# Two fused convolution blocks: raw images in place of normalised ones, and one expert added by an accumulating DMA

## The reference, cut to what matters

```python
def cond_conv(x):                      # x: the group-normalised input
    pooled = mean(x, axis=(2, 3))
    routing = sigmoid(pooled @ w_route.T + b_route)      # (16, 4)
    y = conv3x3(x, w_experts)                            # 4 experts, 128 -> 128
    out = einsum('beohw,be->bohw', y, routing)
    return silu(batch_norm(out))
x = x + cond_conv(group_norm(x))                         # 32 groups of 4 channels
x = x + conv3x3(group_norm(x), sign(W))
```

## Time and profile before

| | us |
|---|---|
| median of 3 runs | 273.05 (272.96 to 273.5) |
| profiled execution, its own time | 273.31 |
| span of its trace | 271.5 |
| PE, DVE, ACT, POOL busy | 264.0, 255.3, 219.6, 43.5 |

### The profile page before, as it was taken

The page is one execution under the profiler, slowest core; times in us unless marked ns, Lnnn a source line. Parts: engine busy times, 40 slices in busy tenths (PEclk is TensorE's granted clock), DMA queues, the critical chain, the costliest instruction groups (busy, mean ns, idle before and its releaser), DMA issues.

```text
span 271.5 us, 4138 instructions
## 1 busy us (share of the span) xinstructions
PE 264.0 (97%) x1339; PEld 183.0 (67%) x1339; DVE 255.3 (94%) x466; ACT 219.6 (81%) x450; POOL 43.5 (16%) x63
## 2 busy tenths in 40 slices
PE   8899999999999999999999999999999999999993
PEld 8544856758485766859586675848576685858663
DVE  5899999999999999999999999999999999995985
ACT  2489988998979798897979799897979895735870
POOL 3011020312112021212112021211202121210110
PEclk9999999999999999999999999999999999999999
DMA  7998836453726545261735545271645536272507
GB/s 215 417 374 304 303 140 154 62 115 72 141 80 96 138 78 154 34 123 78 126 109 77 154 63 121 69 138 77 100 135 77 154 38 121 81 134 97 77 2 155
DMA packets 10245, 35.20 MB, mean 130 GB/s; under 512 B 1264, under 2 KB 1904, under 8 KB 10224
## 3 DMA queue, kind: packets, MB, share of 16 engines
q0 software_dynamic: 4176, 15.21, 33.3%
q1 hardware_dynamic: 5616, 19.34, 18.7%
q10 hardware_dynamic: 432, 0.39, 0.4%
HBM read 11.34 MB, written 16.25 MB: 102 GB/s over the span
## 4 chain that ended last, share of the span: by engine, by line
PE 87%; DVE 8%; ACT 2%; issue 1%; POOL 1%; DVEq 0%; POOLq 0%
PE pc L590 40%; PE pb L555 14%; PE pa L555 14%; PE pe_ L555 13%; DVE U L1163 3%; PE pd L484 2%; PE pd L545 1%; POOL rstd L441 1%; PE ps L524 1%; PE ps L528 1%; DVE e_rows L1194 0%; ACT xn L869 0%; DVE lo L1285 0%; DVE U L1153 0%; DVE even L1172 0%
## 5 line engine op out<-in xcount | busy, mean ns | idle before, releaser
L1163 DVE SCALAR_TENSOR_TENSOR U<-we,route,U 128x1152 f32<-128x1152 f32 x45 | 63.6, 1412 | 0.6
L590 PE MATMUL pc<-lo,ws 128*128 128x496 f16 (+3 forms) x270 | 62.0, 375 | 0.0
L590 PE MATMUL pc<-hi,ws 128*128 128x496 f16 (+3 forms) x270 | 59.8, 375 | 0.5 <-ACT hi L930 0.5
L590 PEld LDWEIGHTS pc<-hi,ws 128*128 128x128 f16 x270 | 26.4, 98 | 30.0 <-issue 0.9
L590 PEld LDWEIGHTS pc<-lo,ws 128*128 128x128 f16 x270 | 27.7, 106 | 26.3
L555 PE MATMUL pb<-V,UM 128*128 128x256 f32 (+1 forms) x180 | 40.6, 375 | 0.6 <-DVE UM L1183 0.6
L555 PE MATMUL pe_<-V,U 128*128 128x256 f32 (+1 forms) x180 | 40.6, 375 | 0.0
L555 PE MATMUL pa<-V,UM 128*128 128x256 f32 (+1 forms) x180 | 40.5, 374 | 0.0
L555 PEld LDWEIGHTS pb<-V,UM 128*128 128x128 f32 x180 | 34.0, 190 | 5.9 <-issue 1.1
L441 POOL TENSOR_TENSOR rstd<-ve,nhalf 128x2 f32<-128x2 f32 (+1 forms) x19 | 15.4, 811 | 139.6 <-ACT ve L845 116.1
L555 PEld LDWEIGHTS pe_<-V,U 128*128 128x128 f32 x180 | 34.1, 190 | 3.8
(11 more groups left out here) (165 smaller groups left out, 408.8 us busy)
## 6 DMA issues: line engine op xcount, KB each, us to landing
X<-x SPq DMA_DIRECT2D x15, 512.0 KB, 5.3
out<-X SPq DMA_DIRECT2D x15, 512.0 KB, 2.6
out<-ev POOLq DMA_DIRECT2D x15, 512.0 KB, 5.5
X<-y POOLq DMA_DIRECT2D x14, 512.0 KB, 4.5
we<-w_experts SPq DMA_DIRECT2D x2, 768.0 KB, 8.4
ws_raw<-w_sign SPq DMA_DIRECT2D x1, 576.0 KB, 10.8
we<-w_experts SPq DMA_DIRECT2D x1, 512.0 KB, 6.4
out<-X SPq DMA_DIRECT2D x1, 384.0 KB, 2.8
```

The source lines that it names most:

```text
L590: mm = mm_(rows[:, r0 - first // W:r1 - first // W, c0:c1], ws[:, tap * C:(tap + 1) * C], plane((hi, lo)[part], i)[:, r0 + ky - 1:r1 + ky ...
L1163: v.scalar_tensor_tensor(out=nine(U[i % RING]), in0=expert(e), scalar=route[:, i, e:e + 1], in1=nine(U[i % RING]), op0=ALU.mult, op1=ALU.a ...
```

## The change

The normalised image is no longer made from image 1 on. The transform reads the raw image from `X`, which now has a row above and below each image; ACT fills these two rows with the group mean (`pads`), and the one point in which the mean does not cancel gets six times the mean added (`centring`). The scale (rstd) goes into the routes, which become rstd x (tanh + 1), with a factor of 0.5 in the batch norm's scale. From image 2 on ACT scales expert 1 into a new tile `scaled` (`scale_second`), POOL issues an accumulating DMA that adds it to `U` (`add_scaled`), and DVE's first mix is that of expert 2 and waits for that DMA. ACT's order becomes: `centring` and `pads` ahead of `hi`, and, behind the SiLU, the statistics of the next image first and then `routing`, `mix` and `scale_second`. In the head the statistics of image 1 move from DVE to ACT, `pool_routes(2)` moves ahead of `mix(1, 3)`, and some small PE products change places.

```diff
-        X = sb("X", [C, B * HW])
+        X = sb("X", [C, B, PH, W])
+        scaled = sb("scaled", [C, K * KCO])
-        xn = [sb(f"xn{p}", [C, PH, W]) for p in range(RING)]
+        xn = sb("xn", [C, PH, W])
...
+        def first_mix(i):
+            return 2 if i >= SCALED_FROM else 1
...
+            def add_scaled(i):
+                pool.wait_ge(mix_first, firsts_before(i) + 1)
+                pool.wait_ge(scaled_ready, i - SCALED_FROM + 1)
+                g.dma_start(flat(U[i % RING][:]), scaled[:], accum_op=ALU.add).then_inc(scaled_added, 16)
...
+            add_scaled(SCALED_FROM)
             for t in range(1, B + 1):
                 power(t + LAG - 1)
                 if 0 <= t - 2 < B - LATE:
                     add_output(t - 2)
                 if ND <= t < B and t not in DVE_RESIDUAL:
                     residual(t)
+                if t + LAG - 1 < B:
+                    add_scaled(t + LAG - 1)
...
+            def centring(i):
+                if in_one(i):
+                    act.wait_ge(gvar_ready, i + 1)
+                else:
+                    act.wait_ge(gnm_ready, gnm_chain(i))
+                for n, factor in enumerate((1.0, P1_SUM)):
+                    activation(centre[:, i, n:n + 1], gnm(i, IN), ACT.Copy, scale=-factor).then_inc(centre_ready, 1)
+            def pads(i):
+                act.wait_ge(centre_ready, 2 * i)
+                activation(X[:, i, 0:PH:PH - 1, :], ones[:, 0:2 * W].rearrange("p (a w) -> p a w", a=2), ACT.Copy,
+                           scale=centre[:, i, 0:1]).then_inc(pads_ready, 1)
...
+            def scale_second(i):
+                wait(act, scaled_added, 16 * (i - SCALED_FROM))
+                activation(scaled[:].rearrange("p (g n) -> p g n", n=C), expert(1), ACT.Copy,
+                           scale=route[:, i, 1:2]).then_inc(scaled_ready, 1)
...
             var_in(3)
+            routing(2)
+            mix(2)
+            scale_second(2)
             silu(0)
             mean_mid(0)
-            routing(2)
-            mix(2)
             squares(LAG)
             add_variance(LAG, IN)
+            sign_weights()
             var_mid(0)
...
                 deviation(c)
+                if c < B:
+                    centring(c)
+                    pads(c)
                 bias(c, MID)
                 split_hi(t - 1)
                 if c < B:
-                    bias(c, IN)
                     pooled_plane(c)
                 split_hn(t - 1)
...
-                if c < B:
-                    normalise(c)
                 if t > 1:
                     silu(t)
                 if 1 < t < B - 1:
                     mean_mid(t)
                 if c + 1 < B:
                     mean_in(c + 1)
-                if c < B:
-                    routing(c)
-                    mix(c)
                 if c + 1 < B:
                     var_in(c + 1)
                 if c + 1 < CHAINS - 1:
                     squares(c + 1)
                 if c + 1 < B:
                     add_variance(c + 1, IN)
+                if c < B:
+                    routing(c)
+                    mix(c)
+                    scale_second(c)
...
-                if e == 1:
+                if e < first_mix(i):
+                    return
+                if e > first_mix(i):
+                    dve.wait_ge(mixed, mixes_before(i) + e - first_mix(i))
+                elif e == 1:
                     dve.wait_ge(mix_first, firsts_before(i) + 1)
                 else:
-                    dve.wait_ge(mixed, mixes_before(i) + e - 1)
+                    dve.wait_ge(scaled_added, 16 * (i - SCALED_FROM + 1))
...
             mix(1, 1)
             mix(1, 2)
+            pool_routes(2)
             mix(1, 3)
-            pool_routes(2)
...
                 if t > 1:
-                    mix(t + 1, 1)
+                    mix(t + 1, 2)
                 inverse_sums(t)
                 inverse_inner(t)
                 inverse_outer(t)
+                if t == 1:
+                    mix(t + 1, 2)
                 pool_routes(t + LAG - 1)
-                if t == 1:
-                    mix(t + 1, 1)
                 low_part(t - 1)
-                mix(t + 1, 2)
                 mix(t + 1, 3)
```

More of the change, by code:

```diff
@@ L33 @@
 K_ZERO, K_INF = -1.5, -6.0
+P1_SUM = 6.0
 G0, G2, G1 = 0, 1, 2
@@ L56 @@
 RING = 3
+SCALED_FROM = 2
 QUARTERS = 4
@@ L127, in build @@
         wroute = sb("wroute", [C, E])
-        parts = {i: sb(f"parts{i}", [C, n, 6]) for i, n in ((0, QUARTERS), (1, 2))}
-        agg = {i: sb(f"agg{i}", [C, 2]) for i in (0, 1)}
+        parts = {i: sb(f"parts{i}", [C, n, 6]) for i, n in ((0, QUARTERS),)}
+        agg = {i: sb(f"agg{i}", [C, 2]) for i in (0,)}
         first_d = sb("first_d", [C, 1])
@@ L277, in mixes_before @@
         def mixes_before(t):
-            return len(DIRECT_PARTS) * (E - 1) * min(t, ND) + (E - 1) * rank(t)
+            return len(DIRECT_PARTS) * (E - 1) * min(t, ND) + sum(E - first_mix(i) for i in range(ND, t))
+        def first_mix(i):
+            return 2 if i >= SCALED_FROM else 1
         def firsts_before(t):
@@ L457, in _ @@
              .then_inc(gdist_ready, 1)
-            for p in range(RING):
-                g.memset(xn[p][:, 0:PH:PH - 1, :], 0.0).then_inc(zeroed, 1)
+            g.memset(xn[:, 0:PH:PH - 1, :], 0.0).then_inc(zeroed, 1)
             g.memset(epsilon[:, 1:2], GN_EPS / LAST_SCALE ** 2).then_inc(zeroed, 1)
@@ L876, in routing @@
                 act.wait_ge(th_ready, i + 1)
-                activation(route[:, i, :], th[:, i, :], ACT.Copy, bias=0.5, scale=0.5).then_inc(route_ready, 1)
+                if i < ND:
+                    activation(route[:, i, :], th[:, i, :], ACT.Copy, bias=0.5, scale=0.5).then_inc(route_ready, 1)
+                else:
+                    act.wait_ge(rstd_ready, i + 1)
+                    activation(route[:, i, :], th[:, i, :], ACT.Identity, bias=rstd[:, i, IN:IN + 1],
+                               scale=rstd[:, i, IN:IN + 1]).then_inc(route_ready, 1)
             def mix(i):
@@ L948, in last_hi @@
                                scale=rstd[:, c, MID:MID + 1]).then_inc(last_hi_ready, 1)
-                activation(last_rest(hi), xn[1][:, LAST_ROWS:H + 1, :], ACT.Copy,
+                activation(last_rest(hi), xn[:, LAST_ROWS:H + 1, :], ACT.Copy,
                            scale=rstd[:, c, MID:MID + 1]).then_inc(last_hi_ready, 1)
@@ L980, in _ @@
             mix_first_part(0, 1)
+            mean_in(1)
             mix_first_part(0, 2)
+            var_in(1)
             deviations(1)
+            centring(1)
             mix_first_part(0, 3)
+            pads(1)
             variance(1)
-            bias(1, IN)
             pooled_plane(1)
-            normalise(1)
+            mean_in(2)
             routing(1)
             mix(1)
-            mean_in(2)
             var_in(2)
             deviations(2)
-            sign_weights()
+            centring(2)
+            mean_in(3)
+            pads(2)
             variance(2)
-            mean_in(3)
-            bias(2, IN)
             pooled_plane(2)
-            normalise(2)
             var_in(3)
+            routing(2)
+            mix(2)
+            scale_second(2)
             silu(0)
             mean_mid(0)
-            routing(2)
-            mix(2)
             squares(LAG)
             add_variance(LAG, IN)
+            sign_weights()
             var_mid(0)
@@ L1201, in inner_rows @@
                     return
-                rows = lambda first: xn[i % RING][:, first:first + H, :].rearrange("p (t k) w -> p t (k w)", k=TROWS)
+                rows = lambda first: X[:, i, first:first + H, :].rearrange("p (t k) w -> p t (k w)", k=TROWS)
                 v.tensor_tensor(f_rows[:].rearrange("p t k w -> p t (k w)"), rows(2)[:, :, W:3 * W],
@@ L1407, in _ @@
                     mix_part(part, x)
-            part_stats(1, 1)
-            aggregate(1)
-            columns(1)
+            bn_factor()
+            bn_scales()
+            bn_offset()
             for x in (1, 2, 3):
                 mix_part(2, x)
-            bn_factor()
-            mix_part(3, 1)
-            bn_scales()
-            mix_part(3, 2)
+            for x in (1, 2, 3):
+                mix_part(3, x)
             pool_routes(1)
-            mix_part(3, 3)
-            bn_offset()
             all_rows(1)
```

62 lines of the change are left out of this document (32 added, 30 removed).

## The result

The changed kernel takes 299.75 us (median of 4 runs, 298.44 to 301.09); the kernel before took 273.15 us beside it (272.96 to 273.5). The ratio is 1.0967, with an interval of 1.095 to 1.0985: 9.7% slower. The profiled execution took 299.47 us, its span is 297.7 us, 26.2 more than before.

A forecast was written before the change was run, and what follows sets the result against it. PE bounds the kernel before at 15.5 us per image; a DMA ring of 17.17 us would replace it. Twelve rounds put PE's late ps 19.1 us later, giving 292.4 us on the profiled execution, 292 as median; range 284 to 308.

The forecast's parts named there:

- What bounds: Kernel before: PE works 15.50 of 15.50 us per image, DVE 15.21, ACT 13.85; PE's head waits total 1.14 us.
- the ring: Scaled tile, POOL's DMA, DVE's mix and inverse transform, ACT up to the next scaled tile: 17.17 us per round.
- The landing: Accumulating DMA from issue to landing: 4.8 us taken, between 4.5 and 4.95; 6.2 us as upper bound.
- The routes: ACT's routes instructions between its mean pass and its mix, within the round: 0.44 us.
- The sum: From SiLU of image 1 through twelve rounds to PE's late ps at 267.5 us, 19.1 us later than before: 292 us.
- the eleven rounds: Eleven of the twelve rounds up to the mix of image 15, expert 2: 17.17 us each.
- the start: First DVE mix of expert 2 that waits for the DMA, image 3: starts at 51.25 us.
- the last, shorter round: Twelfth round, without mean and variance pass because there is no image 16: 14.87 us.
- What would show it: Signs: pb about 17.2 us apart, DVE idle 2 to 3 us, PE about 1.5 at ps and lo, landing 4.8.
- The head: First images: DVE stands 1 us before pooled of image 2, PE starts later; net loss about 0.5 us.
- the wait at 44.19: PE's 0.33 us wait for UM of image 2 in the head, forecast to go.
- ACT's balance: ACT's added and removed work per image: about +0.6 us, inside its 1.65 us of spare time.

The follow-up runs named there:

- the tile later: Changed kernel with scale_second behind the next round's variance of the sum and the DMA issued ahead of power, DVE's wait left early: 323.15 us.
- the half transfer: Changed kernel whose accumulating DMA adds only the first 576 of 1,152 columns, the rest of expert 1 left out: 282.54 us.
- the late wait: Changed kernel with DVE's mix of expert 2 moved from ahead of the inverse transform to behind low_part: 277.39 us.
- another order: Changed kernel with routing, mix and scale_second directly behind the SiLU; DVE's mix of expert 2 then moved behind low_part: 295.38 us before that move, 295.18 after.
- the run that hid it: Changed kernel with DVE's mix of expert 2 behind low_part, scale_second behind the next round's variance of the sum, DMA issued ahead of power: 274.43 us.

## Why the prediction was right, and where its sizes were off

The forecast was 292 us in a range of 284 to 308, on the slower side; 299.75 us were measured. The mechanism was right; the size was 7.75 us short.

*What bounds, and the ring.* Right. It named the ring, its stations and its order, and the runs confirm it from four sides: without the DMA 15.50 us per round, with 1.4 us less landing 1.36 less, with the wait moved 22 us less in all, with the tile later 1.6 more per round.

*The terms of the ring.* The landing, the one term that the trace before did not show, came out at 4.82 us against 4.8. In that there is some luck: 4.8 was chosen between 4.5 and 4.95 with no working of its own, and the growth by bytes behind the 4.95 is steeper than the rows of the half transfer say. The others, read from rows that were there, were off by more. From the scaled tile to POOL's start it takes 0.54 us (117.43 to 117.97), not 0.30: the row used follows SiLU's read of the accumulator, and this one a full pass. The routes take 0.61 us (114.42 to 115.03), not 0.44, since `route<-th,rstd` with its factor takes 0.39 us. DVE's mix takes 1.33 from start to start (105.38 to 106.71), not 1.41, and two small ACT instructions 0.51, not 0.60. Together 17.44, not 17.17. The eleven rounds from DVE's mix at 53.02 to that at 245.87 average 17.53, as a few landings are longer.

*The sum.* `ps` of the last image but one was forecast at 267.5 and runs at 274.20. All of these 6.7 us but 0.9 are mis-sized terms of the sum; the 0.9 come from another holder at the end:

- the eleven rounds, 0.36 us each: 4.0 us, three fifths of the 6.7;
- the start, 53.02 in place of 51.25: 1.8 us. SiLU of image 1 ran 0.6 us later than forecast, ACT's pass from there and POOL's issue took 0.33 us more, and the landing 5.6 us (47.37 to 53.0), not 4.8, with a store issued 0.02 us ahead of it. For the 0.6 us the prediction left out `scale_second(2)`, 1.24 us of ACT's queue ahead of the SiLU of image 0: in the run without scaling and DMA the SiLU of image 1 starts at 38.43 us, here at 39.43 (38.8 forecast);
- the last, shorter round 0.1, and the end 0.9: there PE holds `ps`, not the chain. From the `ps` at 258.75 on PE runs without a wait, 15.45 us of products, up to 274.20:

```profile
258.75 0.35 PE L547 MATMUL ps<-stats,gmat 128*128 128x2 f32 x2 [0.62 <-issue]
...
274.20 0.28 PE L547 MATMUL ps<-stats,gmat 128*128 128x2 f32 x2
```

Behind that `ps` the tail takes 23.5 us, 0.5 more than before. The rest of the 7.75 us is between execution and median: the profiled run lies 0.28 us below its median here and lay 0.26 above it before.

*What would show it.* The landing and SiLU behind the inverse were as announced. DVE's idle time in a round is 3.55 us and not 2 to 3; the prediction's own numbers would have said 3.4: 17.17 us less the 13.80 that DVE still works, which are 15.21 less a mix of 1.41. PE's idle time is 1.5 us, as announced, but at `ps` and, in most rounds, not at `lo`.

*The head.* Its 0.5 us are 0.4 in the kernel without the DMA. The stations are near those forecast:

```profile
24.62 0.22 DVE L1189 SCALAR_TENSOR_TENSOR pooled<-wroute,zr,bshare 128x4 f32<-128x4 f32 x1 [0.83 <-ACT zr L881]
...
27.84 2.77 PE L578 MATMUL pb<-V,UM 128*128 128x256 f32 x12 [0.39 <-DVE UM L1233]
...
37.67 3.97 PE L613 MATMUL pc<-hi,ws 128*128 128x512 f16 x18 [0.83 <-ACT hi L972]
```

DVE's stand is 0.83 us (1 forecast), `pb` of image 1 starts at 27.84 (28.1), `hi` of image 0 at 37.67 (37.05), and the wait at 44.19 is gone.

*ACT's balance.* The step "about +0.6 us per image, inside its 1.65 us" was right in its sum (ACT's busy time per round went from 13.85 to 14.38) and wrong as an argument. It did no harm here, as a longer ring covers it. With that ring open, the late wait shows that `scale_second` lies in the ring through `ps`, which then is 15.68 us long: 0.18 us per image lost, on an engine with time to spare.

## What to carry to other kernels

Where engines run fixed programs and each round hands something to the next, list the rings: every chain that leaves an engine and comes back to it a round later, with all that is queued behind the waiting instruction. The longest ring is the time per round, whatever the busy shares say, and an edit is worth the change of the longest one only: the late wait brought 22 us, and taking away 2.55 us of wait per round in another order brought nothing. A transfer put in place of work on a full engine needs more time between its issue and its use than its landing takes (7.2 us against 5.0 in the run that hid it), neither end may lengthen another ring, and its landing is to be taken with what starts beside it.

## What was not expected of the hardware

The accumulating DMA between two on-chip tiles took 3.4, 4.5 and 4.8 us for 288, 512 and 576 KB; that is an estimated 2.0 us and the bytes at 211 GB/s. Its landing went from 4.8 to 5.6 us where a store began 0.02 or 0.03 us ahead of it, and to 9.4 us in the head, among the loads of `x` (issued at 29.49, landed just before DVE's mix at 38.96). In the run with the scaling later, PE's granted clock is below 0.9 in seven of the page's 40 slices, and seven of the thirteen passes of 17 products of `lo` took 5.17 to 6.58 us in place of 3.78. Ahead of the slow ones PE had stood 0.93 to 2.82 us for `pooled` or `lo`, ahead of the fast ones up to 1.71 us: a wait of 1.71 us ahead of 269.96 left the clock at 1.00, and after one of 0.93 us ahead of 154.59 it is 0.83 over the next stretch. The length of that one wait does not decide; what does stays open.
